# Routing half of a mixture-of-experts layer inside the attention layer before it, the other half as one group; clamp rows of cross attention in four tiles of 32 partitions

## The reference, cut to what matters

```python
x = x + self_attention(layernorm(x));  x = x + cross_attention(layernorm(x), context)
h = layernorm(x)                          # per row
p = softmax(h @ Wg + bg)                  # 8 experts
best two of p, their weights normalised to sum 1
x = x + sum over the two experts e of weight_e * (gelu(h @ W1[e] + b1[e]) @ W2[e] + b2[e])
```

## Time and profile before

| what | value |
|---|---|
| median of 3 runs | 744.03 us (744.03 to 744.82) |
| the profiled execution, its own time | 747.55 us |
| its span, first to last instruction | 745.8 us |
| PE busy | 631.5 us, 85% |
| DVE busy | 459.5 us, 62% |
| ACT busy | 392.6 us, 53% |
| POOL busy | 267.8 us, 36% |
| mean granted clock of TensorE | 0.905 |

### The profile page before, as it was taken

One profiled execution on the slowest core, in us unless ns is written; L12 is line 12 of the kernel. 1 busy time (PEld: TensorE's weight loads), 2 busy tenths in 40 slices (PEclk: granted clock), 3 DMA queues, 4 the chain that ended last, 5 costly groups with the idle time before them and its releaser, 6 DMA issues. The chain is left out here.

```text
span 745.8 us, 17097 instructions
## 1 busy us (share of the span) xinstructions
PE 631.5 (85%) x6411; PEld 449.8 (60%) x6411; DVE 459.5 (62%) x1243; ACT 392.6 (53%) x844; POOL 267.8 (36%) x369
## 2 busy tenths in 40 slices
PE   4899999899999955089999977989999996874876
PEld 2466666556666534047999944667878784442555
DVE  3566756589888848742444425475757565466994
ACT  6567676886777532134344456655565643333432
POOL 4133224344453203760455461051313130244641
PEclk9999999999999965556999996999999998797996
DMA  3023254432122120133666532100000000000000
GB/s 106 2 73 87 63 146 124 113 99 65 43 53 88 43 79 22 51 123 110 221 221 225 188 91 58 55 1 2 2 2 2 2 3 0 1 0 1 15 15 28
DMA packets 53022, 48.94 MB, mean 66 GB/s; under 512 B 10219, under 2 KB 45533, under 8 KB 52685
## 3 DMA queue, kind: packets, MB, share of 16 engines
q1 hardware_dynamic: 47933, 41.94, 18.6%
q0 software_dynamic: 2496, 4.27, 1.8%
q10 hardware_dynamic: 2512, 1.65, 0.9%
HBM read 18.68 MB, written 15.54 MB: 46 GB/s over the span
## 5 line engine op out<-in xcount | busy, mean ns | idle before, releaser
L581 ACT ACTIVATE ptx<-bank 128x512 f32<-128x512 f32 x128 | 66.0, 603 | 69.1 <-PE bank L493 69.1
L1607 POOL COPY ptx<-over_pt 32x512 f32<-32x512 f32 x64 | 39.8, 622 | 121.1 <-DVE over_pt L1573 118.3
L1151 POOL DMA_INDIRECT results<-moe_y,moe_dest x46 | 45.2, 983 | 56.6 <-DVE moe_y L1289 48.8
L393 POOL TENSOR_TENSOR x<-x,l_back 128x128 f32<-128x128 f32 x32 | 14.5, 454 | 109.4 <-ACT l_back L594 94.4
L736 DVE SCALAR_TENSOR_TENSOR ptx<-ptx,bank 128x512 f32<-128x512 f32 x64 | 41.1, 684 | 17.4 <-PE bank L503 16.0
L721 DVE TENSOR_REDUCE l_m<-bank 128x4 f32<-128x512 f32 x64 | 40.9, 678 | 16.5 <-PE bank L477 16.5
L1146 POOL DMA_INDIRECT slots<-xs,moe_pos x32 | 33.8, 1056 | 28.5 <-DVE moe_pos L1232 19.2
L1502 ACT ACTIVATE ke<-bank 64x512 f32<-64x512 f32 x64 | 37.9, 592 | 10.0 <-PE bank L1419 8.9
L721 DVE TENSOR_REDUCE l_m_raw<-bank 128x4 f32<-128x512 f32 x64 | 40.7, 674 | 0.6 <-PE bank L477 0.6
L489 PE MATMUL bank<-ke 32*128 32x512 f32 x256 | 36.5, 639 | 1.1 <-DVE l_m L721 1.1
L521 PE MATMUL bank<-ptx,ke 128*32 128x128 f32 x1024 | 34.7, 276 | 2.3 <-DVE ptx L736 2.2
(11 more groups left out here) (360 smaller groups left out, 1747.7 us busy)
## 6 DMA issues: line engine op xcount, KB each, us to landing
slots<-blank SPq DMA_DIRECT2D x16, 528.0 KB, 4.8
ptx<-w SPq DMA_DIRECT2D x12, 578.0 KB, 3.4
ke<-w SPq DMA_DIRECT2D x11, 578.0 KB, 3.3
w<-in_w SPq DMA_DIRECT2D x16, 256.0 KB
moe_xb<-slots SPq DMA_DIRECT2D x23, 132.0 KB
x<-in_x SPq DMA_DIRECT2D x4, 256.0 KB, 4.7
w<-results SPq DMA_DIRECT2D x4, 256.0 KB, 6.0
w<-results ACTq DMA_DIRECT2D x4, 256.0 KB, 6.0
```

What stands on the lines that cost most here:

```text
L581: nc.scalar.activation(probs[t % 2][:, g, :], score_bank[g][:, :], ACT.Exp, scale=SCALE0).then_inc(s["probs"], 1)
L1151: nc.gpsimd.indirect_dma_start(M.results, bass.IndirectOffsetOnAxis(dest[j % 4][:, n:n + 1], 0), y[j % 4][:, n, :], None, bounds_check=2 * ...
L1607: nc.gpsimd.tensor_copy(ptx[t % 2][r, :, r], pt[t % 2][r, :, :]).then_inc(s["spread"], 1)
```

## The change

Routing is split into two groups of eight batches. The class `Chooser` holds the DVE chain of a group, `group_logits` and `group_ranks` the PE part. The first group runs inside `layer0_attentions`: its normalisation on POOL in steps 27 to 29, its scales on ACT and DVE in steps 24 to 26, transposes on PE in steps 29 and 30, logits in step 30, the choice on DVE in steps 31 and 32, ranks and places behind the last step. The experts' block begins with the 16 scatters of the first group, whose slots are known, while DVE, PE and ACT route the second group. The quantising of weights moves behind the table of blocks on DVE; on ACT `magnitudes(0)` stands ahead of the context chain, `magnitudes(1)` behind its last projection. Buffers move from the block to `build`.

In cross steps `row` and `floor` hold each head group in its own 32 partitions: two rows (high, low) of 512 columns, written by a DMA for each part (four a step instead of two). The four products with `side` then use 32 partitions each. In the diff `N` is 32, `B` 16, `GROUP` 8, `E` 8, `S` 128.

```diff
+def group_logits(nc, M, pe, bank, cols, s, count):
+    o = bank[:, cols].rearrange("p (j e) -> p j e", e=E)
+    nc.tensor.matmul(o, M.ones[0:1, 0:S], M.bg[:, :].rearrange("a (j e) -> a j e", j=1).broadcast_to([1, GROUP, E]),
+                     start=True, stop=False, skip_group_check=True)
+    for j in range(GROUP):
+        if j % 4 == 0:
+            pe.wait_ge(s["xt"], j // 4 + 1)
+        mm = nc.tensor.matmul(o[:, j, :], M.xt[j // 4][:, j % 4 * S:(j % 4 + 1) * S], M.wg[:, :], start=False, stop=j == GROUP - 1,
+                              skip_group_check=True)
+    mm.then_inc(s["logit_ps"], count)
+def group_ranks(nc, M, o, first):
+    last = first + GROUP
+    nc.tensor.matmul(o, M.before[:, :], M.mask[:, first:last, :], start=True, stop=False, skip_group_check=True)
+    for b in range(first):
+        nc.tensor.matmul(o, M.all_ones[:, :], M.mask[:, b:b + 1, :].broadcast_to([S, GROUP, E]), start=False, stop=False, skip_group_check=True)
+    for k in range(GROUP - 1):
+        mm = nc.tensor.matmul(o[:, k + 1:GROUP, :], M.all_ones[:, :], M.mask[:, first + k:first + k + 1, :].broadcast_to([S, GROUP - 1 - k, E]),
+                              start=False, stop=k == GROUP - 2, skip_group_check=True)
+    return mm
...
+    def first_choice(self):
+        V, M, then = self.nc.vector, self.M, self.then
+        self.dve.wait_ge(self.s["exps"], 1)
+        then(V.tensor_reduce(M.r1[:, :, 0], M.p[:, :, :], AX.X, ALU.add))
+        then(V.reciprocal(M.r1[:, :, 0], M.r1[:, :, 0]))
+        then(V.tensor_tensor(M.p[:, :, :], M.p[:, :, :], self.wide(M.r1[:, :, :]), ALU.mult))
+        self.best_of(0)
+        then(V.scalar_tensor_tensor(M.p[:, :, :], M.pair[:, 0, :, :], -2.0, M.p[:, :, :], ALU.mult, ALU.add))
...
+                        high, low = tiles(row[p])
+                        wait(sp, s["mt_hi"], u, plus=1)
+                        sp.dma_start(high.bitcast(F32), mt[0:H, :].bitcast(F32)).then_inc(s["row"], 16)
                         wait(sp, s["mt"], u, plus=1)
-                        sp.dma_start(row[p][0:3, :].bitcast(F32), mt[0:MT, :].bitcast(F32)).then_inc(s["row"], 16)
+                        sp.dma_start(low.bitcast(F32), mt[32:MT, :].bitcast(F32)).then_inc(s["row"], 16)
+                        high, low = tiles(floor[p])
                         wait(sp, s["l_ps"], u, per=NG, plus=-NG)
+                        wait(sp, s["lt_hi"], u, plus=1)
+                        sp.dma_start(high.bitcast(F32), lt_parts[0:H, :].bitcast(F32)).then_inc(s["lrow"], 16)
                         wait(sp, s["lt_lo"], u, plus=1)
-                        sp.dma_start(floor[p][0:3, :].bitcast(F32), lt_parts[0:MT, :].bitcast(F32)).then_inc(s["lrow"], 16)
+                        sp.dma_start(low.bitcast(F32), lt_parts[32:MT, :].bitcast(F32)).then_inc(s["lrow"], 16)
...
+                    for b in {27: (0, 1), 28: (2, 3, 4), 29: (5, 6, 7)}.get(t, ()):
+                        routed_rows(b)
...
-                    wait(pe, s["row"], t, per=16, plus=16)
+                    pe.wait_ge(s["row"], rows(t))
                     for g in range(NG):
-                        nc.tensor.matmul(score_bank[g][:, :], weights(t).side[:, :], row[t % 2][:, g * 512:(g + 1) * 512],
+                        r, c = slice(0, 128), slice(512 * g, 512 * g + 512)
+                        if cross(t):
+                            r, c = slice(32 * g, 32 * g + 32), slice(0, 512)
+                        nc.tensor.matmul(score_bank[g][:, :], weights(t).side[r, :], row[t % 2][r, c],
                                          start=False, stop=True, skip_group_check=True).then_inc(s["st_ps"], 1)
...
+                        r = slice(32 * g, 32 * g + 32)
+                        nc.tensor.matmul(floor_bank[g][:, :], weights(t).side[r, :], floor[t % 2][r, :],
                                          start=True, stop=True).then_inc(s["l_ps"], 1)
+                def turn_routed(q):
+                    wait(pe, s["xt"], q)
+                    for j in range(4):
+                        wait(pe, s["rows"], q, per=4, plus=j + 1)
+                        mm = nc.tensor.transpose(front_bank[:, j * S:(j + 1) * S], M.xs[:, 4 * q + j, 0:D], ident[:, :])
+                    mm.then_inc(s["xt_ps"], 1)
...
                     wait(pe, s["back"], backs(t))
+                    if t == N - 2:
+                        pe.wait_ge(s["next"], 16 * (5 + 2 * E))
+                        group_logits(nc, M, pe, pv_bank, slice(3 * S, 3 * S + GROUP * E), s, 1)
...
                     front_part(t)
+                    if t in (N - 3, N - 2):
+                        turn_routed(t - (N - 3))
...
+                pe.wait_ge(s["mask"], 1)
+                pe.wait_ge(s["prepared"], 6)
+                pe.wait_ge(s["patterns"], 1)
+                pe.wait_ge(s["back"], backs(N))
+                group_ranks(nc, M, ranks, 0).then_inc(s["rank_ps"], 1)
...
+                    if t == N - 7:
+                        act.wait_ge(s["variance"], 1)
+                        nc.scalar.activation(M.root[:, 0:GROUP], M.rstd[:, 0:GROUP, 0], ACT.Sqrt).then_inc(s["root"], 1)
+                    if t in (N - 3, N - 2):
+                        q = t - (N - 3)
+                        act.wait_ge(s["xt_ps"], q + 1)
+                        nc.scalar.activation(M.xt[q][:, :], front_bank[:, :], ACT.Copy).then_inc(s["xt"], 1)
...
+                    if t == N - 1:
+                        chooser.shifted(logits)
                     if b:
                         weighted(t - 1)
+                    if t == N:
+                        chooser.second_choice()
...
+                    if t == N - 3:
+                        routing_constants()
+                    if t == N - 1:
+                        chooser.first_choice()
...
+                chooser.place(ranks)
                 dve.wait_ge(s["aggr1"], N)
+                dve.wait_ge(s["ready"], 1)
...
+                group_logits(nc, M, pe, logit_bank, slice(0, GROUP * E), s, 1)
+                pe.wait_ge(s["mask"], 1)
+                group_ranks(nc, M, by_expert(rank_bank), GROUP).then_inc(s["rank_ps"], 1)
...
+                nc.scalar.activation(M.root[:, GROUP:], M.rstd[:, GROUP:, 0], ACT.Sqrt).then_inc(s["root"], 1)
+                for q in range(2):
+                    wait(act, s["xt_ps"], q, plus=1)
+                    nc.scalar.activation(xt[q][:, :], turn[q][:, :], ACT.Copy).then_inc(s["xt"], 1)
+                act.wait_ge(s["shifted"], 1)
+                nc.scalar.activation(M.p[:, :, :], M.z[:, :, :], ACT.Exp).then_inc(s["exps"], 1)
+                for n in range(3):
+                    nc.scalar.activation(M.over_hi[:, n, :], M.over_w[:, n, :], ACT.Copy).then_inc(s["high"], 1)
+                magnitudes(0)
...
+                magnitudes(1)
...
-                for q in range(NB):
-                    pool.wait_ge(s["ready"], q + 1)
-                    for j in range(4):
-                        for k in range(2):
-                            nc.gpsimd.indirect_dma_start(M.slots, bass.IndirectOffsetOnAxis(pos[:, k, 4 * q + j:4 * q + j + 1], 0),
-                                                         M.xs[:, 4 * q + j, :], None).then_inc(s["scattered"], 16)
+                for b in range(B):
+                    if b == GROUP:
+                        pool.wait_ge(s["ready"], 1)
+                    for k in range(2):
+                        nc.gpsimd.indirect_dma_start(M.slots, bass.IndirectOffsetOnAxis(pos[:, k, b:b + 1], 0),
+                                                     M.xs[:, b, :], None).then_inc(s["scattered"], 16)
...
+                chooser.shifted(by_expert(logit_bank))
+                chooser.first_choice()
+                chooser.second_choice()
+                chooser.place(by_expert(rank_bank))
+                constants()
                 blocks()
                 for n in range(3):
                     dve.wait_ge(s["high"], n + 1)
                     V.tensor_tensor(M.over_lo[:, n, :], M.over_w[:, n, :], M.over_hi[:, n, :].bitcast(F32), ALU.subtract).then_inc(s["low"], 1)
+                prepare(0, range(SIGNED_STEPS))
+                prepare(1, range(SIGNED_STEPS))
```

More of the change, by code:

```diff
@@ L238, in layer0_attentions @@
             smax_ps maxed m_clip back_ps back mt_hi mt row st_ps probs pv rden o_norm x_done
-            cross_weights cross_prepared next lt_hi lt_lo lt lrow l_ps clipped biased blank filled later""")
+            cross_weights cross_prepared next lt_hi lt_lo lt lrow l_ps clipped biased blank filled later
+            variance root rstd rows xt_ps xt logit_ps shifted exps step mask rank_ps ready patterns consts_int""")
         N = 2 * B
@@ L268, in layer0_attentions @@
         FIRST = -4
+        logits, ranks = [pv_bank[:, c:c + GROUP * E].rearrange("p (j e) -> p j e", e=E) for c in (3 * S, 3 * S + GROUP * E)]
         def fronts(t):
@@ L278, in sums, with rows, tiles @@
             return t + 4
+        def rows(t):
+            return 16 * (t + 1 + max(0, t + 1 - B))
```

(33 more changed lines are left out.)

222 lines of the change are left out of this document (77 added, 145 removed).

## The result

Changed kernel: 758.48 us median of 4 runs (758.35, 748.71, 758.61, 758.92), against 744.42 for the kernel before: ratio 1.016, 95% interval 1.0097 to 1.0223 (ratios are formed over the single runs; the two medians alone give 1.019). The forecast was 729.7 us in a range of 723.5 to 735. The profiled execution took 758.35 us. A run more than 1.5% above the fastest of its kernel is left out of the ratios in this document.

What follows compares the result with a forecast made beforehand. PE was taken to bound the cross steps, POOL's scatter path the routing, with the context chain close behind. Layer 0 +1.5 and scatters -19.8 make -18.3; 744.03 - 18.3 + 4.0 = 729.7 us, range 723.5 to 735.

Steps and rivals of the forecast that it cites:

- The context chain must follow.: Routing stage: context chain ends 47 to 48 us behind the block's start, against 48.3 for the scatters, so it fits.
- If the timed runs have no such hole.: Kernel before, routing: if timed runs lack the profiled 4.33 us wait of POOL for DVE's places, they gain 4.0 less.
- The rival with the right mechanism: Second group's ranks: a 6 us hole makes the context chain end last, at 53, +4.7, 734.4 us; chance 0.1.
- Layer 0, +1.5 in all: First layer: 2.4 + 1.9 + 1.1 + 0.3 us longer, less 4.2 from the tiles.
- The tail on DVE: Layer 0's end: 11 choice operations, statistics and five of places behind L746 end at 274.1 instead of 272.27, +1.9 us.
- The table-load step: Step 25: ACT's square root and exponential need two table loads, so the step takes 8.68 us against 7.59, +1.1.
- Step 30: Layer 0: PE waits for ACT's second copy of turned rows, then eight logit products; values and everything behind start 2.4 us later.
- The tiles' -4.2: Cross steps: side products as tiles of 32 rows save 0.3 us a step in 14 steps.
- The first scatter: Experts' block: POOL's first scatter starts within 1 us of the block's start, since the first group is already routed.
- 32 scatters: Routing stage: POOL issues all 32 in one row without a wait, ended 43 us later, at 1.35 each.
- the second group ready before POOL asks: Routing stage: second group ready 17 to 18.5 us behind the block's start, 3 to 4.5 before POOL needs it.
- The rival of slower scatters: Routing stage: all 32 scatters take 0.26 us more, beside DVE's quantising, +8.3 less the old share, 736 us; chance 0.04.

Runs made afterwards that it cites:

- E1: Changed kernel, but POOL waits for the counts before its 17th scatter, on the first chip: 732.39 us, 0.9887 of the kernel before.
- E9: Changed kernel with POOL waiting for the counts before its 17th scatter, on the third chip: 739.4 us, 0.9909 of the kernel before.
- E14: Changed kernel with only POOL's wait for the counts, on the fifth chip: 737.29 us, 0.989 of the kernel before.
- E16: Changed kernel with POOL's wait for the counts and two buffers for the cross steps' context, sixth chip: 739.49 us, 0.9892 of the kernel before.
- E13: Changed kernel with POOL's wait for the counts and each floor product of a cross step issued twice, fifth chip: 740.67 us, 0.9938 of the kernel before.
- E17: Changed kernel with only POOL's wait for the counts, on the sixth chip: 738.37 us, 0.9874 of the kernel before.
- E5: The changed kernel unedited, on the second chip: 761.2 us beside 746.13 for the kernel before; no ratio given.
- E8: The changed kernel unedited, on the third chip: 760.53 us, 1.0173 of the kernel before.
- E15: The changed kernel unedited, on the fifth chip: 755.89 us, 1.015 of the kernel before.
- E4: Kernel before with only the tiles of 32 in the cross steps, routing as before, first chip: 738.81 us, 1.0005 of the kernel before.
- E12: Changed kernel with POOL's wait for the counts and weights quantised ahead of the table, fourth chip: 736.33 us, 0.9954 of the kernel before.

## Why the prediction was wrong, by its own steps

- **The step that failed: "The context chain must follow." and its end, "It fits, with 0.5 to 1.5 to spare."** It summed durations of work, 47 to 48 behind the block's start. The chain ended 74.1 behind it (354.26 - 280.19). Without held increments the sum would have done: in E1 it ended 43.4 behind the block's start and the rows' fetch decided, at 331.48. The missing term is the wait for the counts' held-up increment (23.17, after 7.80 for the ranks), and the Abs pass that carries it on to the context: the copy starts 9.7 behind the transposes' first increment.
- **"If the timed runs have no such hole."** The earlier trace rows was this very effect, small: PE done at 317.97, DVE served at 324.04. It began in the midst of scatters and ended 2.9 behind the last of them:

```profile
318.47 0.16 DVE L1219 TENSOR_TENSOR moe_best<-moe_best 128x4 f32<-128x4 f32 x1
...
319.69 0.17 DVE L1220 TENSOR_TENSOR xs<-moe_best,moe_r 128x4 f32<-128x4 f32 x1 [1.05 <-DVE moe_best L1219]
320.14 0.96 POOL L1146 DMA_INDIRECT slots<-xs,moe_pos  x1 [0.30 <-issue]
```

  I explained it away by a difference of 3.5 us between one execution and a median. The rival with the right mechanism ("32 short mask products stand there together now") had a chance of 0.1 and a price of 4.7, because I moved the old hole unchanged to a new place. The old one was short, by all that E9 shows, because the eight scatters of the third group ran out and POOL then stood still, waiting for DVE; the change removes just that pause. E9 puts it back.
- **Layer 0, +1.5 in all, was +6.3** (block start 280.19 against 273.93). The tail on DVE was right: +1.9, though the terms given for it add up to 1.8. The table-load step was right, 8.83 for 8.68. Step 30 was about right: the scores of step 31 start 2.6 later, at 262.94 against 260.33. A term was missing behind it: these scores (L611) ran at half clock (0.50 from 262 to 265) and took 2.09, where L489 takes 1.14, and by the last division the delay is 3.9 (L901 at 273.58 against L746 at 269.68). From DVE's end to the block's start it is 0.5 more. The tiles' -4.2 became nothing: from the first row transfer of the cross steps to the last, table loads included, the change takes 118.1 (140.26 to 258.40), the kernel before 116.7, and the last one is issued at 258.40 in both. Eight steady steps gained 0.35 to 0.44 each, but the steps from 147.47 to 158.15 and from 166.84 to 177.34 took 10.7 and 10.5, against 9.0 and 7.6, partly at half clock. SP's timeline of the change, first row transfer of each step:

```profile
147.47 0.54 SPq L401 DMA_DIRECT2D over_xlo<-l_mt  x1
158.15 0.53 SPq L401 DMA_DIRECT2D over_xhi<-l_mt  x1
166.84 0.53 SPq L401 DMA_DIRECT2D over_xlo<-l_mt  x1
177.34 0.53 SPq L401 DMA_DIRECT2D over_xhi<-l_mt  x1
184.50 0.53 SPq L401 DMA_DIRECT2D over_xlo<-l_mt  x1
191.66 0.53 SPq L401 DMA_DIRECT2D over_xhi<-l_mt  x1
```

  PE had waited 2.25 and 1.96 for the context's load just before these stretches at half clock, where the kernel before waits 1.28 and 0.56; whether that wait has a part in it is open (E14, E16). A gain in the steady step is not yet a gain of the stage: two longer steps took back what eight shorter ones gave.
- **The first scatter** was to start with the block; it started 2.50 behind it, and 2.5 to 2.9 behind it in every trace of the change and its variants. Nothing in the traces accounts for that.
- **Right:** 32 scatters in 41.0 us for the forecast 43.1, the second group ready before POOL asks where nothing is held up (15.6 behind the block in E1, forecast 17 to 18.5; in the change the late ranks made POOL wait 0.86), no late row transfers and late floor transfers in three steps only (1.0 us in all in the list of waits of L629), a steady period of 7.16 for "near 7.3" (L618 now starts 0.56 behind L611, where L493 started 1.07 behind L489). With the wait of POOL the kernel measures 0.987 to 0.991 of before; the forecast was 0.981. The difference, 4.5 to 7.4 us, is of the size of layer 0's 4.8 too much and the 2.5; this is a sum, not an experiment.

The rival of slower scatters was no part of it: in the changed kernel DVE's long operations come behind the scatters, and every scatter but the first takes 0.95 or 0.96. In E9 the two scatters beside DVE's low halves took 1.79 and 1.97, two later ones 1.63 and 1.68: some 3 us of 46, as much as in the kernel before, where four take 1.56 to 1.96. The 1.22 that the prediction laid on the quantising is the first scatter's own: it takes 1.24 here, with no quantising beside it. The Trainium skill, SBUF — State Buffer, section SBUF: two separate sides, says that one pair of ports is an exclusive lock between VectorE and GpSimd, and that a VectorE operation with two inputs in SBUF takes it against a GpSimd operation that reads SBUF. The rows 1.79 and 1.97 agree in that they are longer; a lock they do not show.

## What to carry to other kernels

If a consumer's row starts microseconds behind its producer's last row, with no row between, that time is a term of the path: find what runs beside it, and ask whether the change makes that run longer. Before removing the pauses of an engine that issues indirect transfers back to back, look at what used to get through in them; a wait of 3 us placed on purpose was worth 19 to 21 us on the two chips where both kernels ran beside each other. And where a long chain is released by one increment, don't queue a second chain behind it on another engine.

## What was not expected of the hardware

PE's semaphore increments can arrive 33 us behind the products (294.80 and 327.44), while POOL issues an indirect DMA every 1.26 us, and 2.5 to 2.9 us behind the last scatter once it pauses (E9, E13, E14, E16, E17). Without a pause they come 3.8 to 4.9 behind the last scatter of all (the change, E5, E8), but not always: in E15 DVE takes the counts at 320.31, 1 us before it ends. DVE's own increments are touched too: in the kernel before, two DVE operations that follow one another, the first 0.16 long, stand 1.2 apart just before the hole of the earlier trace rows (318.47 and 319.69). The profiled executions show late increments on five of seven occasions (the result, and the second, third, fifth and sixth chip) and not on two (E1 to E4, and E12), and where it is there not every run of the change is long (748.71 and 742.84 among runs near 760).

What is full, if anything is, is not shown. Every run of the change and its variants, the timed ones too, has the profiler's span and clock on record, so none tells whether the hold-up exists without them. The Trainium skill's page NOTIFIC — the notification-queue block, section 7.1 Overflow: three behaviours, one of which stalls the engine, says that the block that writes such records pushes back on its producers when its internal pipeline is full. That would fit a crowd of short products beside transfers that each leave many records; no run here shows it.
